# Placing stage of a graph network kernel: three of eight tiles picked on ScalarE, and SyncE's order of broadcasts and stores

## The chip, the cores and the metric

The kernel runs on one core of one Trainium2 chip. The time is device microseconds of one launch. Before the change three runs took 3246.53, 3248.45 and 3257.93 us; the median is 3248.45 us.

## The reference

100000 nodes with 64 features, 50000 edges (`src`, `dst`), `dst` sorted. A first layer takes a maximum over edges, a second one a normalised sum over edges, five times, each followed by a layer norm. Cut to what matters here:

```python
# layer 0: maximum over the edges of each target node
h = relu(concat([x[tgt], x[src] - x[tgt]], axis=1) @ W + b)
x = layernorm(x + maximum(segment_max(h, tgt), 0))
# layer 1: degree norm, then five sums over edges, mixed with six coefficients
deg  = segment_sum(ones, col);  inv = where(isinf(deg ** -0.5), 0, deg ** -0.5)
norm = inv[row] * inv[col]
for k in range(1, 6):
    tx = segment_sum(norm[:, None] * tx[col], row)
    result = result + coeffs[k] * tx
x = layernorm(x + result)
```

To do this in dense passes the kernel first sorts the edges by their first endpoint itself: it gives every edge a position, and writes the edge's record (64 features, two ids) to that position of a table in HBM. The stage that finds positions and writes records is the placing stage, and it alone is changed.

## The kernel before

`count_and_place` (L193) has four blocks of engine programs: reading the ids, counting, flags, and placing (L706 to L953). Then come a barrier and `edge_pass` and the sums.

**The data of the placing stage.** Edges stand in 392 tiles of 128. They are done four at a time, in 98 turns; turn (i, s) takes tiles of half s, with i from 0 to 48 and s 0 or 1. A node number is split in a high part (which of 250 rows) and a low part (which of 400 columns). `tps[s]` holds in PSUM, for half s, the next free position of every node (125 partitions, two times 400). Each turn of PE does, in this order:

- L858: for each of four tiles j, four matmuls of 400 columns pick the row of each edge's node out of `table[:, s]` into the bank `gps[j]`. The table is given in two bf16 parts, a high and a low one, for two halves of the rows. Ahead of tile j it waits for `got_read[j]`, that is, until the bank was read in the turn before.
- L836, ahead of tile 2: two matmuls take the high part away from `tps` of the other half, so that ACT can read the low part; and after tile 3 two more add the high part back for this half.
- L865: eight matmuls add the four tiles' one-hot rows to `tps[s]`, after `onehots[s]`; then `added[s]`.

**DVE** in a turn (L803): `ranks` of the next turn (L769, four comparisons with a row sum), `positions` of the turn before (L801, waits for all four `got_read` and writes `pos`), `hots` of the next turn (L779, L780, eight one-hot rows), then `pick` of this turn (L792): for each of four tiles it multiplies the 400 columns of `gps[j]` by the one-hot row of the low part and sums, which leaves the edge's position in `at[:, s, j]`.

**ACT** in a turn: `high` (L891, copies `tps` as bf16, after `added`), `rows` (L876 twice, L880: from a broadcast row `hibc` to the transposed one-hot rows `hiT`), `low` (L895), `factor` (L885, 32 numbers for each partition into `wide[s]`, after the load `wide_in[s]`, then `wide_ready[s]`).

**POOL** (L948) scatters four tiles by indirect DMA after `pos_ready`.

**SP** issues all plain DMAs of the stage from one in-order queue: `rows` (L725: two broadcasts `hibc` and `srcbc` of 256 KB, once `rows_used` from DVE's ranks and `dist_done` from ACT allow), `widened` (stores `wide[s]` to `x_ext`, after `wide_ready`), `widen` (loads `wide[s]` with node features, after `wide_stored`). A load or store is two DMAs, partitions 0 to 111 and 112 to 124 (`node_dma`, L127, so that their line in the profile is L130). This side job makes a copy of the node features with their factors, 100 pieces in all, and has nothing to do with the positions; it shares the ACT and SP programs. `wide` has two buffers.

Of the kernel before, what the change touches and what calls it, by code (L numbers as in the profile page):

```python
# [30 lines left out]
ACT = mybir.ActivationFunctionType  # L31
# [10 lines left out]
NEG = -1e30  # L42
ROUND = 12582912.0
FAR = float(1 << 20)

NP = 125
NC = N // NP
# [145 lines left out]
def count_and_place(nc, d, k):  # L193

    with ExitStack() as scope:
# [480 lines left out]
        front.close()  # L676
        two = lambda name: [sem(f"{name}{s}") for s in range(2)]
        rows_in, rows_used, dist_done, hiT_ready = two("rows_in"), two("rows_used"), two("dist_done"), two("hiT_ready")
        onehots, added, table_ready = two("onehots"), two("added"), two("table_ready")
        pos_ready = two("pos_ready")  # L680
        got, got_read = [sem(f"got{j}") for j in range(4)], [sem(f"got_read{j}") for j in range(4)]
# [5 lines left out]
        with ExitStack() as inner:  # L687
            isb = lambda name, shape, dt=FP32: inner.enter_context(nc.sbuf_tensor(name, shape, dt))
            hibc, srcbc = isb("hibc", [P, 2, GPOS]), isb("srcbc", [P, 2, GPOS])
            dist = isb("dist", [NP, 2, GPOS])  # L690
            hiT = isb("hiT", [NP, 2, 2, GPOS], BF16)
            ohp = isb("ohp2", [P, 2, 4, NROW], BF16)
            ohc = isb("ohc2", [P, 2, 4, NR], BF16)

# [14 lines left out]
            @block.sync  # L709
            def _(sp):  # L710
                by_column = (d.x.rearrange("(p c) f -> p c f", c=NC), d.x_ext[0:N, :].rearrange("(p c) f -> p c f", c=NC))

                def widen(i, s):
                    before, = settle(sp, k, i * 32)
                    sp.wait_ge(wide_stored[s], before)
                    cols = ds(i * (2 * KN) + s * KN, KN)
                    node_dma(sp, wide_in[s], lambda a, b: wide[a:b, s, :, 0:C], lambda a, b: by_column[0][a:b, cols, :])

                def widened(i, s):
                    again, = settle(sp, k, i + 1)  # L720
                    sp.wait_ge(wide_ready[s], again)
                    cols = ds(i * (2 * KN) + s * KN, KN)
                    node_dma(sp, wide_stored[s], lambda a, b: by_column[1][a:b, cols, :], lambda a, b: wide[a:b, s])

                def rows(i, s):  # L725
                    before, twice = settle(sp, k, i, i * 2)
                    sp.wait_ge(rows_used[s], before)
                    sp.wait_ge(dist_done[s], twice)
                    for to, of in ((hibc, d.hi_rows), (srcbc, d.src_rows)):
                        sp.dma_start(to[:, s], of[ds(i * GPOS + s * (ET // 2 * P), GPOS)].partition_broadcast(P)  # L730
                                     ).then_inc(rows_in[s], 16)

                for s in range(2):
                    rows(0, s)
                sp.dma_start(d.factor.rearrange("(p c) f -> p (c f)", c=NC), k.D[:]).then_inc(factor_stored, 16)
                sp.wait_ge(wide_blank, 1)
                for s in range(2):
                    widen(0, s)
                rows(1, 0)
                widened(0, 0)  # L740
                rows(1, 1)
                widened(0, 1)
                widen(1, 0)
                with sp.Fori(1, LAST) as i:
                    rows(i + 1, 0)
                    widened(i, 0)
                    widen(i, 1)
                    rows(i + 1, 1)
                    widened(i, 1)
                    widen(i + 1, 0)  # L750
                widened(LAST, 0)
                widen(LAST, 1)
                widened(LAST, 1)
                widen(LAST + 1, 0)
                widened(LAST + 1, 0)
                widen(LAST + 1, 1)
                widened(LAST + 1, 1)
                for s in range(2):
                    sp.wait_ge(wide_stored[s], (EB // 2 + 1) * 32)
                sp.wait_ge(factor_stored, 16)  # L760

            @block.vector
            def _(dve):
# [23 lines left out]
                def pick(i, s):  # L787

                    dve.wait_ge(onehots[s], i + 1)
                    for j in range(4):  # L790
                        dve.wait_ge(got[j], i * 2 + s + 1)
                        dve.scalar_tensor_tensor(picked[:, j], gps[j][:, 0:NR], 1.0, ohc[:, s, j],  # L792
                                                 ALU.mult, ALU.mult, accum_out=at[:, s, j:j + 1]
                                                 ).then_inc(got_read[j], 1)
# [36 lines left out]
            @block.tensor  # L831
            def _(pe):
                def high_part(s, sign):

                    for h in range(2):
                        last = pe.matmul(tps[s][:, h, 0:NR], eye[:, sign], table[:, s, 0, h],  # L836
                                         start=False, stop=True, skip_group_check=True)
                    return last

                for s in range(2):  # L840
                    for h in range(2):
                        last = pe.matmul(tps[s][:, h, 0:NR], k.ident[0:NP, 0:NP], start[:, s, h * NR:(h + 1) * NR],
                                         start=True, stop=True)
                last.then_inc(seeded, 1)
                pe.wait_ge(high_ready[0], 1)
                high_part(0, 1).then_inc(low_left[0], 1)
                with pe.Fori(0, EB // 2) as i:
                    for s in range(2):
                        pe.wait_ge(hiT_ready[s], i + 1)
                        pe.wait_ge(table_ready[s], i + 1)  # L850
                        for j in range(4):
                            if j == 2:
                                pe.wait_ge(high_ready[1 - s], i + s + 1)
                                high_part(1 - s, 1).then_inc(low_left[1 - s], 1)
                            pe.wait_ge(got_read[j], i * 2 + s)
                            for h in range(2):
                                for w in range(2):
                                    last = pe.matmul(gps[j][:, 0:NR], hiT[:, s, h, j * P:(j + 1) * P], table[:, s, w, h],  # L858
                                                     start=h + w == 0, stop=h + w == 2)
                            last.then_inc(got[j], 1)  # L860
                        high_part(s, 0)
                        pe.wait_ge(onehots[s], i + 1)
                        for j in range(4):
                            for h in range(2):
                                last = pe.matmul(tps[s][:, h, 0:NR], ohp[:, s, j, h::2], ohc[:, s, j],  # L865
                                                 start=False, stop=True, skip_group_check=True)
                        last.then_inc(added[s], 1)

            @block.scalar
            def _(act):  # L870
                def rows(i, s):

                    act.wait_ge(rows_in[s], i * 32 + 32)
                    act.wait_ge(hiT_ready[1 - s], i + s)
                    for h in range(2):
                        act.activation(dist[:, h], hibc[0:NP, s], ACT.Abs, bias=part[0:NP, h:h + 1]  # L876
                                       ).then_inc(dist_done[s], 1)
                    act.wait_ge(dist_done[s], i * 2 + 2)
                    act.wait_ge(added[s], i)
                    act.activation(hiT[:, s], dist[:], ACT.Relu, bias=1.0, scale=-1.0).then_inc(hiT_ready[s], 1)  # L880

                def factor(i, s):
                    act.wait_ge(wide_in[s], i * 32 + 32)
                    act.wait_ge(nd_ready, 1)
                    act.activation(wide[:, s, :, D_COL:], nd_all[:, ds(i * (2 * KN) + s * KN, KN), :], ACT.Copy  # L885
                                   ).then_inc(wide_ready[s], 1)
# [9 lines left out]

                for sign in range(2):
                    act.activation(eye[:, sign], k.ident[0:NP, 0:NP], ACT.Copy, scale=1.0 - 2.0 * sign)
                rows(0, 0)
                act.wait_ge(seeded, 1)  # L900
                high(0, 0)
                low(0, 0)
                with act.Fori(0, LAST) as i:
                    for s in range(2):
                        high(1 - s, i + s)
                        rows(i + s, 1 - s)
                        low(1 - s, i + s)
                        factor(i, s)
                high(1, LAST)
                rows(LAST, 1)  # L910
                low(1, LAST)
                factor(LAST, 0)
                high(0, LAST + 1)
                factor(LAST, 1)
                for s in range(2):
                    factor(LAST + 1, s)
# [1129 lines left out]
```

## Time and profile before

The profiled execution took 3252.13 us (its span is 3250.4 us), 3.7 us above the median of the three runs.

| engine | busy us | share of span |
|---|---|---|
| PE matmul | 1783.3 | 55% |
| DVE | 2578.0 | 79% |
| ACT | 1964.3 | 60% |
| POOL | 2228.1 | 69% |

The placing block runs from about 669 us to the first instruction of the next block at 1270.30 us. Shares over the whole span are means over many stages; for this change only the stretch of the placing stage is to be read, and in it which wait ends last.

### The profile page before, as it was taken

How to read it: one execution, taken by the hardware profiler on the slowest of the kernel's cores; microseconds unless marked ns; L12 is line 12 of the kernel's file. 1: busy time of each engine (PE TensorE's matmuls, PEld its weight loads, DVE VectorE, ACT ScalarE, POOL GpSimd, SP SyncE). 2: the span in 40 equal slices, each digit the busy share in tenths (PEclk: the TensorE clock that was granted, in tenths of full speed). 3: DMA queues.
4: the chain of work that ended last, by engine and by line, in shares of the span. 5: the costliest groups of instructions: out<-in, count | busy, mean ns of one | idle time of the engine just before them, and what ended most of it. 6: DMA issues, size and time to landing. Idle time of an engine off the chain costs nothing. (4 is left out here: it accounts for less than half of the span.)

```text
span 3250.4 us, 66637 instructions
## 1 busy us (share of the span) xinstructions
PE 1783.3 (55%) x9465; PEld 1075.8 (33%) x9465; DVE 2578.0 (79%) x12074; ACT 1964.3 (60%) x4437; POOL 2228.1 (69%) x2285
## 2 busy tenths in 40 slices
PE   7995555468888885988888883433333332000000
PEld 6884444335555553444444441111111111000000
DVE  8996999999999996899899996455556666555554
ACT  7995877556666663789888883255545400444443
POOL 6777777057777776577777775676666665777776
PEclk9998999989999997689888885555555555555555
DMA  4311444157777775688888885766667633222221
GB/s 142 109 24 23 116 109 108 52 142 202 204 203 203 204 202 126 170 211 221 203 214 212 214 208 112 175 177 181 174 156 202 169 92 79 69 69 70 74 74 53
DMA packets 736782, 467.28 MB, mean 144 GB/s; under 512 B 411287, under 2 KB 622546, under 8 KB 736728
## 3 DMA queue, kind: packets, MB, share of 16 engines
q1 hardware_dynamic: 636084, 321.23, 36.9%
q0 software_dynamic: 75296, 92.22, 13.3%
q10 hardware_dynamic: 25348, 53.33, 5.4%
q14 instruction: 48, 0.39, 0.0%
q8 instruction: 6, 0.10, 0.0%
HBM read 271.38 MB, written 197.86 MB: 144 GB/s over the span
## 5 line engine op out<-in xcount | busy, mean ns | idle before, releaser
L1647 POOL DMA_INDIRECT rows_H<-tab,at_H x424 | 404.2, 953 | 215.8 <-DVE at_H L1700 113.1
L948 POOL DMA_INDIRECT rec<-edge_x,pos x392 | 412.1, 1051 | 163.2 <-issue 159.3
L1150 POOL DMA_INDIRECT rows_M<-x_ext,at_M x400 | 379.4, 948 | 150.0 <-issue 100.0
L1922 POOL DMA_INDIRECT out_x<-res_L,to_L x384 | 374.2, 975 | 119.3 <-issue 107.0
L1668 ACT ACTIVATE node_H<-node_H,mean,M2n 125x64 f32<-125x64 f32 x800 | 273.6, 426 | 259.2 <-issue 152.6
L1808 PE MATMUL zT_H<-ident,z_H 128*64 128x128 f32 x496 | 150.3, 407 | 444.7 <-issue 351.9
L858 PE MATMUL gps<-table,hiT 125*128 125x400 bf16 x1568 | 300.8, 335 | 92.1 <-DVE picked L792 91.0
L377 POOL DMA_INDIRECT edge_x<-in_x,x_at x196 | 204.3, 1043 | 70.0 <-issue 58.8
L543 POOL DMA_INDIRECT edge_x<-in_x,x_at x196 | 187.7, 958 | 67.7 <-issue 59.4
L596 PE MATMUL aps<-ohc_f,ohp_f 128*125 128x400 bf16 x784 | 155.4, 341 | 130.3 <-DVE ohp_f L517 130.3
L1939 ACT ACTIVATE std_L<-M_L,coef 128x2 f32<-128x2 f32 x192 | 56.7, 295 | 274.9 <-DVE M_L L2001 274.7
L858 PEld LDWEIGHTS gps<-table,hiT 125*128 125x128 bf16 x1568 | 146.2, 98 | 222.6 <-DVE picked L792 125.3
L365 DVE TENSOR_SCALAR ohc<-iota,lo 128x400 bf16<-128x400 f16 x784 | 216.5, 317 | 0.0
L1808 PEld LDWEIGHTS zT_H<-ident,z_H 128*64 128x64 f32 x496 | 45.5, 140 | 484.7 <-issue 484.2
L792 DVE SCALAR_TENSOR_TENSOR picked<-gps,ohc 128x400 bf16<-128x400 f32 x392 | 200.4, 563 | 0.0
L449 PE MATMUL cps<-ohc,ohp 128*125 128x400 bf16 x784 | 198.1, 335 | 2.9 <-ACT ohd L414 2.6
L449 PE MATMUL cps<-ohc,ohd 128*125 128x400 bf16 x784 | 197.8, 334 | 0.0
L769 DVE SCALAR_TENSOR_TENSOR eq<-srcbc,recs,mask 128x128 bf16<-128x128 f32 (+3 forms) x392 | 194.1, 546 | 0.1
L891 ACT ACTIVATE table<-tps 125x800 bf16<-125x800 f32 x99 | 82.9, 837 | 170.6 <-PE tps L865 170.6
L1747 DVE TENSOR_TENSOR_SCAN sums_H<-cont,sums_H,zT_H 64x256 f32<-64x256 f32 (+1 forms) x248 | 182.2, 735 | 1.1 <-issue 0.6
L409 ACT ACTIVATE far<-iota,hi 128x250 f32<-128x250 f16 x392 | 163.6, 488 | 12.2 <-issue 12.2
L1157 POOL DMA_INDIRECT Ds<-factor,to x138 | 139.0, 1007 | 42.1 <-issue 41.5
(323 smaller groups left out, 5946.0 us busy)
## 6 DMA issues: line engine op xcount, KB each, us to landing
tab<-given_M SPq DMA_DIRECT2D x98, 384.0 KB
hibc_f<-dst_hi_rows SPq DMA_DIRECT2D x98, 256.0 KB
hibc<-hi_rows SPq DMA_DIRECT2D x98, 256.0 KB
srcbc<-src_rows SPq DMA_DIRECT2D x98, 256.0 KB
tab<-given_M SPq DMA_DIRECT2D x98, 256.0 KB
own<-given_M SPq DMA_DIRECT2D x98, 256.0 KB
own_L<-own SPq DMA_DIRECT2D x192, 128.0 KB
x_ext<-wide SPq DMA_DIRECT2D x100, 241.5 KB
```

Source lines behind the costliest of these rows:

```text
L365: last = dve.tensor_scalar(ohc[:, u, j, w], k.iota[:], lo[:, w, t], None, ALU.is_equal)
L377: pool.indirect_dma_start(out=edge_x[:, t // 4, t % 4, 0:C], out_offset=None, in_=d.x, in_offset=bass.IndirectOffsetOnAxis(ap=x_at[:, t:t ...
L449: last = pe.matmul(cps[2 if w else j // 2][:, h, 0:NR], rows[:, u, j, h::2], ohc[:, u, j, w], start=False, stop=True, skip_group_check=True)
L769: last = dve.scalar_tensor_tensor(eq[:, j, 0:n], srcbc[:, s, 0:n], recs[:, t, 1], mask[:, GPOS - n:GPOS], ALU.is_equal, ALU.mult, accum_ou ...
L792: dve.scalar_tensor_tensor(picked[:, j], gps[j][:, 0:NR], 1.0, ohc[:, s, j], ALU.mult, ALU.mult, accum_out=at[:, s, j:j + 1]).then_inc(got ...
L858: last = pe.matmul(gps[j][:, 0:NR], hiT[:, s, h, j * P:(j + 1) * P], table[:, s, w, h], start=h + w == 0, stop=h + w == 2)
L948: pool.indirect_dma_start(out=d.rec, out_offset=bass.IndirectOffsetOnAxis(ap=pos[:, s, j:j + 1], axis=0), in_=edge_x[:, i + s * (EB // 2), ...
L1150: pool.indirect_dma_start(out=rows[:, s, j, :], out_offset=None, in_=d.x_ext, in_offset=bass.IndirectOffsetOnAxis(ap=at[:, s, j:j + 1], ax ...
L1647: pool.indirect_dma_start(out=rows[:, s, j, :], out_offset=None, in_=gather, in_offset=bass.IndirectOffsetOnAxis(ap=at[:, s, j:j + 1], axi ...
L1668: last = act.activation(node[:, s, j], node[:, s, j], ACT.Identity, scale=k.M2n[:, col], bias=k.mean2[:, col])
L1808: last = pe.transpose(zT[s][:, j * P:(j + 1) * P], z[:, s, j, :], k.ident[:])
L1922: pool.indirect_dma_start(out=d.out, out_offset=bass.IndirectOffsetOnAxis(ap=to[:, s, j:j + 1], axis=0), in_=res[:, s, j, :], in_offset=No ...
```

## The change

PE adds, to the banks of three of eight tiles, 131072 times the one-hot row of the low part (one more matmul of 400 columns for each of them, with `lift`, a scaled unit matrix in bf16). The wanted column then stands 131072 above all others, and a relu of (value - 131072) with row sum on ACT gives the position. ACT does this for tiles 2 and 3 when s is 0 and for tile 3 when s is 1, between `low` and `factor`; DVE picks the others. PE now waits for `onehots[s]` ahead of the first lifted tile. In SP's program the broadcasts of a half are issued one half turn sooner: `rows(i+2, 0)` ahead of `widened(i, 1)` where `rows(i+1, 1)` stood, and so on. ACT makes `lift` and `lower` (the bias) once, at the start.

```diff
+LIFT = 131072.0
+ON_ACT = ((2, 3), (3,))
+ON_DVE = tuple(tuple(j for j in range(4) if j not in a) for a in ON_ACT)
@@ sync
                 rows(1, 0)
+                rows(1, 1)
                 widened(0, 0)
-                rows(1, 1)
+                rows(2, 0)
                 widened(0, 1)
                 widen(1, 0)
-                with sp.Fori(1, LAST) as i:
-                    rows(i + 1, 0)
+                with sp.Fori(1, LAST - 1) as i:
+                    rows(i + 1, 1)
                     widened(i, 0)
                     widen(i, 1)
-                    rows(i + 1, 1)
+                    rows(i + 2, 0)
                     widened(i, 1)
                     widen(i + 1, 0)
+                rows(LAST, 1)
+                widened(LAST - 1, 0)
+                widen(LAST - 1, 1)
+                widened(LAST - 1, 1)
+                widen(LAST, 0)
@@ vector, pick
-                    for j in range(4):
+                    for j in ON_DVE[s]:
@@ tensor
+                pe.wait_ge(lift_ready, 1)
...
-                                                     start=h + w == 0, stop=h + w == 2)
+                                                     start=h + w == 0, stop=h + w == 2 and j in ON_DVE[s])
+                            if j in ON_ACT[s]:
+                                pe.wait_ge(onehots[s], i + 1)
+                                last = pe.matmul(gps[j][:, 0:NR], lift[:], ohc[:, s, j], start=False, stop=True)
                             last.then_inc(got[j], 1)
@@ scalar
+                def pick(i, s):
+                    act.wait_ge(pos_ready[s], i)
+                    for n, j in enumerate(ON_ACT[s]):
+                        act.wait_ge(got[j], i * 2 + s + 1)
+                        act.activation(raised[:, n], gps[j][:, 0:NR], ACT.Relu, bias=lower[:],
+                                       accum_out=at[:, s, j:j + 1]).then_inc(got_read[j], 1)
+                act.activation(lift[:], k.ident[:], ACT.Copy, scale=LIFT).then_inc(lift_ready, 1)
+                act.activation(lower[:], k.ones[:, 0:1], ACT.Copy, scale=-LIFT).then_inc(lowered, 1)
...
                         low(1 - s, i + s)
+                        pick(i, s)
                         factor(i, s)
...
                 low(1, LAST)
+                pick(LAST, 0)
                 factor(LAST, 0)
                 high(0, LAST + 1)
+                pick(LAST, 1)
                 factor(LAST, 1)
```

## Rows read from the trace of the kernel before

**Rows 1.** Busy time by stretch: PE, PEld, DVE, ACT, POOL, clock, DMA share, GB/s
```profile
900.00:1000.00 100.00, 83.89 (x480) 53.47 (x479) 100.00 (x445) 68.31 (x104) 72.44 (x69) 1.00 0.77 204
```

**Rows 2.** Waits from 700 to 1240 us: who waited for whom, total, times, longest
```profile
ACT table L891 <- PE tps L865: 161.8, 92, 1.9
...
ACT wide L885 <- DMA wide<-in_x: 5.7, 15, 0.8
...
SPq L721 <- ACT wide L885: 198.0, 92, 3.2
```

**Rows 3.** Instructions in order of time, DVE in one turn: start, length, instruction, idle
```profile
903.03 0.56 DVE L792 SCALAR_TENSOR_TENSOR picked<-gps,ohc 128x400 bf16<-128x400 f32 x1
...
905.00 0.34 DVE L769 SCALAR_TENSOR_TENSOR eq<-srcbc,recs,mask 128x128 bf16<-128x128 f32 x1
...
906.89 0.15 DVE L801 TENSOR_TENSOR pos<-at,base 128x4 uint32<-128x4 f32 x1
...
908.89 0.56 DVE L792 SCALAR_TENSOR_TENSOR picked<-gps,ohc 128x400 bf16<-128x400 f32 x1
```

**Rows 4.** Instructions in order of time, ACT and PE in the same turn
```profile
902.74 0.84 ACT L891 ACTIVATE table<-tps 125x800 bf16<-125x800 f32 x1 [1.87 <-PE tps L865]
...
903.66 1.53 PE L858 MATMUL gps<-table,hiT 125*128 125x400 bf16 x8 [0.96 <-DVE picked L792]
...
905.79 0.82 ACT L895 ACTIVATE table<-tps 125x800 bf16<-125x800 f32 x1
...
906.50 0.22 ACT L885 ACTIVATE wide<-nd_all 125x32 f32 x1
...
908.61 0.84 ACT L891 ACTIVATE table<-tps 125x800 bf16<-125x800 f32 x1 [1.88 <-PE tps L865]
...
909.34 1.32 ACT L876 ACTIVATE dist<-hibc,part 125x512 f32<-125x512 f32 x2
```

**Rows 5.** Instructions in order of time, POOL at the end of the stage
```profile
1260.66 0.97 POOL L948 DMA_INDIRECT rec<-edge_x,pos  x1 [0.30 <-issue]
1261.93 0.97 POOL L948 DMA_INDIRECT rec<-edge_x,pos  x1 [0.31 <-issue]
```

**Rows 6.** Instructions in order of time, the factor on ACT and SP's issues
```profile
696.05 0.23 ACT L885 ACTIVATE wide<-nd_all 125x32 f32 x1 [0.24 <-DMA wide<-in_x]
...
696.51 0.93 SPq L130 DMA_DIRECT2D x_ext<-wide  x2
...
697.77 1.03 SPq L130 DMA_DIRECT2D wide<-in_x  x2
...
702.39 0.23 ACT L885 ACTIVATE wide<-nd_all 125x32 f32 x1 [0.35 <-DMA wide<-in_x]
...
725.04 0.23 ACT L885 ACTIVATE wide<-nd_all 125x32 f32 x1 [0.23 <-DMA wide<-in_x]
...
902.31 1.02 SPq L130 DMA_DIRECT2D wide<-in_x  x2
...
903.93 0.35 SPq L730 DMA_DIRECT2D hibc<-hi_rows  x1
```

**Rows 7.** Instructions in order of time, the same at the end of the stage
```profile
1252.71 0.99 SPq L130 DMA_DIRECT2D wide<-in_x  x2
...
1256.13 0.23 ACT L885 ACTIVATE wide<-nd_all 125x32 f32<-125x32 f32 x1 [4.37 <-DMA wide<-in_x]
...
1260.94 0.23 ACT L885 ACTIVATE wide<-nd_all 125x32 f32<-125x32 f32 x1 [4.57 <-DMA wide<-in_x]
```

**Rows 8.** Groups of ACT instructions by line and shape: busy, mean ns, idle before
```profile
L876 ACT ACTIVATE dist<-hibc,part 125x512 f32<-125x512 f32 x196 | 129.7, 711 | 5.8 <-DMA srcbc<-src_rows 5.8
...
L281 ACT ACTIVATE coef<-ones 128x1 f32<-128x1 f32 x1 | 0.2, 203 | 1.8 <-POOL ones L265 1.8
```

**Rows 9.** Instructions in order of time, a pair of broadcasts with nothing behind it
```profile
679.06 0.35 SPq L730 DMA_DIRECT2D hibc<-hi_rows  x1
```

**Rows 10.** Busy time by stretch, the end of that pair's transfers (columns of rows 1)
```profile
682.90:683.15 0.25, 0.25 (x3) 0.07 (x2) 0.25 (x3) 0.13 (x1) 0.19 (x1) 0.50 0.07 25
```

More of the change, by code:

```diff
@@ L678, in count_and_place @@
         rows_in, rows_used, dist_done, hiT_ready = two("rows_in"), two("rows_used"), two("dist_done"), two("hiT_ready")
+        lift_ready, lowered = sem("lift_ready"), sem("lowered")
         onehots, added, table_ready = two("onehots"), two("added"), two("table_ready")
@@ L691, in count_and_place @@
             hiT = isb("hiT", [NP, 2, 2, GPOS], BF16)
+            lift, lower = isb("lift", [P, P], BF16), isb("lower", [P, 1])
+            raised = isb("raised", [P, 2, NR])
             ohp = isb("ohp2", [P, 2, 4, NROW], BF16)
@@ L898, in _ @@
                     act.activation(eye[:, sign], k.ident[0:NP, 0:NP], ACT.Copy, scale=1.0 - 2.0 * sign)
+                act.activation(lift[:], k.ident[:], ACT.Copy, scale=LIFT).then_inc(lift_ready, 1)
+                act.activation(lower[:], k.ones[:, 0:1], ACT.Copy, scale=-LIFT).then_inc(lowered, 1)
                 rows(0, 0)
+                act.wait_ge(lowered, 1)
                 act.wait_ge(seeded, 1)
```

## The prediction

> **What bounds the kernel now.** I read the views from coarse to fine. Busy time by stretch comes first: in the placing stage DVE is busy 100.00 of 100 us, PE 83.89, POOL 72.44 and ACT 68.31, and PE runs at its full granted clock, 1.00 [rows 1]. So DVE has no idle time to give, and the others do. The list of waits says the same from the other side: ACT waits 161.8 us in 92 turns for PE's last matmuls [rows 2]. But ACT's list has a second line, which counts here: 15 times of 92 it waits for the load of `wide`, 5.7 us in all. And SP waits 198.0 us for ACT's factor [rows 2]. These two belong to one chain, and I come back to it.
>
> Then one turn in order of time. From pick to pick DVE's turn is 908.89 - 903.03 = 5.86 us [rows 3]. The four picks take from 903.03 to 905.00, that is 1.97 us or 0.49 us each (less than the 0.56 us of one instruction, since they overlap); the ranks take from 905.00 to 906.89, 1.9 us; the rest is positions and one-hot rows. ACT works from 902.74 to 906.72 (3.98 us) and then waits 1.88 us for PE [rows 4]. PE starts at 903.66, after 0.96 us of waiting for DVE's picks, and is done shortly before 908.61, when ACT's next copy starts [rows 4]: some 4.9 us for 28 matmuls, 0.17 us each. There are 98 turns.
>
> **The change part by part.**
>
> *DVE loses three picks of eight.* Two turns cost 11.72 us now, and 3 x 0.49 = 1.48 us go: 10.24 us, 5.12 us a turn in the mean. The edit has nothing else on DVE. If DVE stayed the bound, 95 turns in the loop would give 95 x 0.74 = 70 us. The question is what is late next.
>
> *PE gains three matmuls in two turns.* At 0.17 us each a turn has 28 plus 1.5, about 5.0 to 5.1 us. This takes up most of PE's idle time but stays below DVE's new 5.12. The new wait for `onehots[s]` costs nothing: DVE makes these rows ahead of the picks of the turn before, and PE itself waits for the first of those picks before it starts its turn [rows 4]. Behind that wait are the turn's other matmuls; nobody else is held.
>
> *POOL.* Where it is not kept waiting, its scatters follow each other by 1261.93 - 1260.66 = 1.27 us [rows 5]; four are 5.1 us. So POOL too could follow down to 5.1 and no further. It doesn't bind at a slower pace.
>
> *ACT gains three picks in two turns.* No relu with row sum is in the trace. The nearest row is L876, which has a bias operand as the pick has and 512 columns where the pick has 400: 0.711 us [rows 8], and the pair of them takes 1.32 us [rows 4], so that the first takes a slot of 0.61 us. Below that lies a half of the 800-column copy, 0.41 us [rows 4]. The row sum may be read out in an instruction of its own, as on DVE; the smallest ACT instruction takes 0.203 us [rows 8]. The bounds are thus 0.41 and 0.71 + 0.20 = 0.91 us; I take 0.7, near the slot of L876 with part of a read-out. ACT's turn is then 3.98 + 1.4 = 5.4 us with two picks and 4.7 with one, 5.8 and 4.9 at the upper bound. In the mean ACT is just below DVE's 5.12 too. ACT's 1.88 us of idle time covers the picks now; with a shorter turn the cover is all but used up.
>
> For this the rows say: a pick is 0.49 us on DVE and 0.6 or more on ACT, so moved work gets dearer, but it goes from an engine that never idles to one that waits 1.88 us a turn. The Trainium skill, page "ScalarE: Activation LUTs", section "Rules for kernel authors", advises VectorE and not ScalarE for a relu or a multiplication. By that rule alone the move would be a loss of 0.1 to 0.2 us an operation; the trace bears out the dearer price, and the busy shares speak for the move all the same.
>
> *The chain that becomes the bound: the side copy.* The factor of a turn needs the load of its `wide` buffer. SP issues that load only behind the store of the turn before, and this store waits for that turn's factor. So factor leads to factor: in the free-running start the factor ran at 696.05, the store was issued at 696.51, the next load at 697.77, and the next factor ran when it had landed, at 702.39 [rows 6]. The first part is 697.77 - 696.05 = 1.72 us and is the same in the new program. The landing took 4.62 us here. From 696.05 to 725.04 are five turns, each of which ended in such a wait; the first two and the last stand in [rows 6]; so the chain ran at 5.80 us a turn without being held by anything else, which leaves 4.08 us for a mean landing. At the end of the stage, with no broadcasts beside it, the landing took 1256.13 - 1252.71 = 3.42 us, and the whole chain 1260.94 - 1256.13 = 4.81 us [rows 7]. In mid-stage the load is issued at 902.31 and the factor comes at 906.50 without waiting, so it has landed within 4.19 us [rows 4, 6], as it had in 77 of 92 turns [rows 2].
>
> So this chain runs today at nearly the pace of DVE, 5.8 against 5.86 us; ACT's slack hides it. Once DVE and ACT could go at 5.1 it can't hide any more, because the factor now stands at the very end of an ACT program without slack, and the next `high` is queued behind it: then PE, then all others. The bounds of its turn are 1.72 + 3.42 = 5.14 us (nothing beside it) and 5.80 (the free start). The broadcasts are beside it all the time, so I stay near the upper end; but 77 of 92 turns without a wait show landings below the early mean. I take a landing of 3.98 us and a turn of 5.70 us.
>
> *SP's order.* The broadcasts of a half are needed by ACT at 909.34 and issued at 903.93 [rows 4, 6], 5.4 us ahead; at a turn of 5.70 they would have 0.3 us less in the old order. In the new order they have a turn more. What they are moved past is one store and one load. The kinds in the queue follow each other as before (broadcasts, store, load, broadcasts), only one half turn ahead in index, so each load still has the same bytes before it. The added wait is on `rows_used` of one turn later; queued behind it on SP are the store and the load. In a turn bound by the side chain DVE has 0.5 us of idle time and its ranks are done before SP comes to them, so I cost it at nothing; the second rival is what it costs otherwise.
>
> *Start and end.* Two small ACT instructions at the start (0.2 to 0.8 us) lie beside DVE's set-up. `rows(1, 1)` ahead of the first store may delay the side chain by a microsecond. At the end the side chain has three turns of about 4.8 us as before.
>
> **The sum.** 95 turns x (5.86 - 5.70) = 15 us. The profiled execution of 3252.1 us would become 3237; it lies 3.7 above the median of the runs, so against 3248.45 I forecast 3233 us. With 5.60 it is 25 us (3223), with 5.80 it is 6 us (3242).
>
> **The rivals.**
>
> *First: the side chain gives way (faster).* If the loads land in 3.4 to 3.8 us, as at the stage's end, the chain runs at 5.1 to 5.5 us, and DVE's 5.12, POOL's 5.1 or ACT set the pace. For it: 3.42 us [rows 7]. Against it: the early turns, and a DMA share of 0.77 that would rise to 0.85 or more in a shorter turn [rows 1]. Gain 95 x 0.36 to 0.74 = 34 to 70 us: 3178 to 3214. Chance 0.17.
>
> *Second: SP's new wait lands on the side chain (slower).* Today the ranks end at 906.89, 0.4 us after the factor at 906.50 [rows 3, 4]. If DVE keeps that lag, SP comes to the broadcasts, waits for the ranks, issues two broadcasts (about 0.9 us) and only then the store: 1.3 us after the factor in place of 0.46, so 0.9 us more in each turn of the chain. Worse, the store's data could queue behind the broadcasts': a lone pair issued at 679.06 was still moving at 682.9 [rows 9, 10], almost 4 us, of which up to 3 would lie ahead of the store. The full price can't persist, since a turn longer by so much lets DVE catch up; a quarter to a half microsecond over today's turn could. This decides from the point where the broadcasts are issued less than about 3 us ahead of the store. At 6.0 to 6.3 us a turn it costs 13 to 42 us: 3261 to 3290. Against it: nothing in the sum keeps DVE late, once it has slack. Chance 0.18.
>
> The Trainium skill, page "DMA: Bandwidth & Descriptors", section "Queues, rings and completion order", says that each DMA engine takes its descriptors in ring order. By that rule broadcasts issued just ahead of a store do stand before it, which is what this rival needs; no row here shows the order by itself.
>
> *Third: ACT's picks are dear, or the chain stays at its early pace (no change).* At 0.91 us a pick the turn with two is 5.8 us and the other is bound by the load at 5.7 to 5.8: 3240 to 3252. Chance 0.15.
>
> **How the numbers follow.** The forecast's own case, a turn of 5.60 to 5.80 us, has 0.50 and spans 3223 to 3242; the first rival 0.17, the second 0.18, the third 0.15. A measurement of this kernel can tell about 0.5% from no change, that is 16 us, or 3232. The forecast's case is cut in half by that line. Faster: 0.17 + 0.25 = 0.42. Within 0.5%: 0.25 + 0.15 = 0.40. Slower: 0.18. The range of 8 in 10 leaves out about half of each outer rival: 3195 to 3266.
>
> **What would show it.** In the new profile the turn from `high` to `high` should be 5.7 us; DVE's busy share in the stage should fall to about 90% and it should wait for ACT's picks or PE; ACT's wait for PE should nearly vanish and its wait for the load of `wide` should grow from 5.7 us to tens of us in most turns; an ACT pick should be near 0.6 to 0.7 us. If instead DVE stays at 100% with a turn near 5.15, the first rival is right. If the broadcasts are issued right after the end of DVE's ranks and the store right behind them, with a load landing over 4.5 us after its issue, it is the second. What would make me wrong is above all the landing time of the load: 0.1 us of it is 9.5 us of the result.

## The result, and the profile after

The changed kernel takes 3226.69 us (median of 7 runs, 3216.22 to 3234.35), the kernel before 3248.45 us (median of 7). The ratio is 0.9927, with a 95% interval of 0.9904 to 0.9949: about 24 us faster, between 17 and 31. The forecast was 3233 us, 15 us faster.

The placing block, from its first POOL instruction to the first one of the next block, went from 1270.30 - 669.42 = 600.9 us to 1243.50 - 669.65 = 573.9 us in the profiled executions, 27.0 us. The first instruction of the next block, before and changed (start, length, instruction, idle before it):

```profile
1270.30 0.10 POOL L1163 MEMSET d_got_M<- 128x3 f32 x1 [7.39 <-POOLq L97]
...
1243.50 0.10 POOL L1192 MEMSET d_got_M<- 128x3 f32 x1 [9.03 <-POOLq L100]
```

The two spans differ by 34.4 us. The other 7 us lie in blocks that the change doesn't touch; more on that at the end. The profiled execution of the changed kernel, 3217.72 us, is also 9 us shorter than the median of its runs. A turn, from one `high` of ACT to the next, took 5.86 us in the mean and takes 5.61 (90 turns from 702.67 to 1207.53 us); 95 turns of that are 24 us, and the other 3 of the 27 us lie ahead of these turns or behind them.

Busy time by stretch, changed kernel, columns as in rows 1:

```profile
900.00:1000.00 100.00, 92.07 (x526) 58.23 (x524) 92.60 (x411) 86.46 (x161) 72.19 (x73) 1.00 0.76 212
```

DVE is no longer full. PE rose from 84 to 92 us and ACT from 68 to 86. POOL did not move, 72.19 for 72.44, although its scatters in 100 us rose from 69 to 73, as the shorter turns want: one of them is shorter now, 0.99 us in the mean for 1.05. The waits from 700 to 1230 us (who waited for whom, total, times, longest), first of PE, ACT, DVE and POOL, then SP's:

```profile
POOL rec L977 <- issue: 128.4, 365, 3.3
PEld tps L848 <- ACT table L914: 71.0, 89, 2.2
ACT wide L908 <- DMA wide<-in_x: 61.1, 74, 2.2
...
DVE pos L813 <- ACT raised L902: 33.9, 38, 2.2
POOL rec L977 <- DVE pos L813: 14.6, 17, 1.5
```

```profile
SPq L727 <- ACT wide L908: 177.4, 94, 3.2
```

ACT's 161.8 us of waits for PE [rows 2] are gone, and the line for the load of `wide` has grown from 5.7 us in 15 turns to 61.1 us in 74. What stands behind it in the list is its echo: PE waits for ACT's `high`, which is queued behind the factor; DVE waits for ACT's picks. Two turns in order of time, ACT and SP:

```profile
899.19 1.02 SPq L133 DMA_DIRECT2D wide<-in_x  x2
...
901.37 0.59 ACT L902 ACTIVATE raised<-gps,lower 128x400 f32<-128x400 f32 x1
901.85 0.20 ACT L902 ACTIVATION_READ_ACCUMULATOR raised<-gps,lower 128x1 f32 x1
903.73 0.23 ACT L908 ACTIVATE wide<-nd_all 125x32 f32 x1 [1.68 <-DMA wide<-in_x]
904.04 0.84 ACT L914 ACTIVATE table<-tps 125x800 bf16<-125x800 f32 x1
904.16 0.92 SPq L133 DMA_DIRECT2D x_ext<-wide  x2
...
905.40 1.00 SPq L133 DMA_DIRECT2D wide<-in_x  x2
...
907.80 0.59 ACT L902 ACTIVATE raised<-gps,lower 128x400 f32<-128x400 f32 x1
...
908.37 0.59 ACT L902 ACTIVATE raised<-gps,lower 128x400 f32<-128x400 f32 x1
...
909.12 0.23 ACT L908 ACTIVATE wide<-nd_all 125x32 f32 x1
909.25 0.82 ACT L914 ACTIVATE table<-tps 125x800 bf16<-125x800 f32 x1
```

The turn with one pick waits for its load: issued at 899.19, factor at 903.73, a landing of 4.54 us ("landing" is the time from the issue of the load to the factor that waited for it). This one is long: in the 74 turns that waited the mean is 3.97 us, from 3.34 to 5.11. The turn with two picks has ACT at work from 904.04 to 909.25 without a gap, 5.21 us. From factor to load issue it is 905.40 - 903.73 = 1.67 us (mean of 95 turns 1.68, and 1.68 in the kernel before in the same stretch; [rows 6] has 1.72). The two picks with their read-outs take 909.12 - 907.80 = 1.32 us, 0.66 each.

### The profile page after: what moved, and what is told of

Read it like the earlier page. It is cut to its first block and busy times, and to the rows that moved or that the text cites. A ratio compares the mean times of both kernels' runs of the same rounds, so it can differ in the third digit from the quotient of the medians.

```text
span 3216.0 us, 67050 instructions
## 1 busy us (share of the span) xinstructions
PE 1807.6 (56%) x9612; PEld 1089.5 (34%) x9612; DVE 2510.0 (78%) x11780; ACT 2051.7 (64%) x4733; POOL 2210.8 (69%) x2285
## 5 line engine op out<-in xcount | busy, mean ns | idle before, releaser
L977 POOL DMA_INDIRECT rec<-edge_x,pos x392 | 398.5, 1016 | 148.3 <-issue 131.2
L871 PEld LDWEIGHTS gps<-table,hiT 125*128 125x128 bf16 x1568 | 153.2, 98 | 109.3 <-issue 3.4
L1737 DVE SCALAR_TENSOR_TENSOR value_H<-rows_H,coef 128x128 f32<-128x128 f32 x212 | 73.3, 346 | 113.1 <-DMA rows_H<-tab,at_H 112.0
L559 ACT ACTIVATE dist_f<-hibc_f,part 125x512 f32<-125x512 f32 x196 | 130.8, 714 | 41.3 <-DMA hibc_f<-dst_hi_rows 35.2
```

Of the source, the lines that this page charges most:

```text
L977: pool.indirect_dma_start(out=d.rec, out_offset=bass.IndirectOffsetOnAxis(ap=pos[:, s, j:j + 1], axis=0), in_=edge_x[:, i + s * (EB // 2), ...
```

## The experiments

The ratios are to runs of the kernel before on the same chip. "Turn" is the mean of 90 turns of ACT; "stage" is the placing block as above, in the profiled execution; "scatters" is from the first to the last start on POOL's scatter line. Two kernels that leave the fourth tile's scatters for later ran once each and are read for their turns only.

| kernel | ratio to before (95%) | turn us | stage us | scatters us |
|---|---|---|---|---|
| before | 1 | 5.86 | 600.9 | 570.8 |
| changed | 0.9927 (0.9904 to 0.9949) | 5.61 | 573.9 | 543.2 |
| picks_only | 1.0034 (1.0010 to 1.0059) | 6.02 | 613.3 | 584.3 |
| order_only | 0.9993 (0.9974 to 1.0013) | 5.87 | 601.6 | 570.7 |
| two_picks | 0.9903 (0.9877 to 0.9930) | 5.64 | 576.2 | 545.4 |
| load_first | 0.9914 (0.9883 to 0.9945) | 5.54 | 568.3 | 539.3 |
| two_picks_load_first | 0.9892 (0.9858 to 0.9927) | 5.52 | 567.0 | 536.9 |
| deep_pos | 0.9849 (0.9823 to 0.9874) | 5.47 | 564.4 | 535.4 |
| three_buffers | 0.9883 (0.9863 to 0.9903) | 5.51 | 565.3 | 536.2 |
| three_buffers_deep_pos | 0.9911 (0.9893 to 0.9928) | 5.12 | 569.8 | 540.7 |

### The two halves of the change

**picks_only**: the picks are moved, SP keeps the order of the kernel before.

> Only the picks are moved; SP keeps its old order. Side-chain theory: the chain of the side copy is the same and runs at 5.6 us a turn; the broadcasts come 5.4 us ahead at a turn of 5.86 and 5.1 us ahead at 5.6, with a landing of about 5 us, so ACT waits for some of them, 0 to 0.3 us a turn: ratio 0.993 to 0.999. Rival, the new order brings most of the gain: ratio 1.000 or above. Rival, the new order is of no use: 0.9927 as the whole change.

It is slower than the kernel before, 1.0034, where 0.993 to 0.999 was expected: the number is that of the rival in which the new order brings the gain. The wait was foreseen, its price wasn't: ACT and DVE both wait for the broadcasts, in most turns.

```profile
DVE eq L775 <- DMA srcbc<-src_rows: 66.2, 75, 1.9
ACT dist L886 <- DMA srcbc<-src_rows: 65.2, 70, 1.9
```

(Waits of picks_only from 700 to 1200 us.) The lead, from the issue of the broadcasts to ACT's first use, was 5.48 us in the mean before ([rows 4, 6] show one of 5.4), and 2 of 85 turns waited. Here it is 4.74 us and 70 turns wait. In the old order the broadcasts stand behind the store and the load, these stand behind the factor, and the factor now stands behind the picks.

**order_only**: DVE picks all tiles, SP has the new order.

> Only SP's order is changed; DVE picks all eight tiles. DVE stays the bound at 5.86 us a turn. Theory of the prediction's second rival: DVE's ranks end 0.4 us after the factor, so the broadcasts and behind them the store are issued up to 0.9 us later than now; the side chain then takes 5.8 + 0.3 to 0.9 us and takes the pace over: turn 5.9 to 6.2, ratio 1.002 to 1.010. Rival, the wait costs nothing since ACT's slack of 1.9 us covers a later load: turn 5.86, ratio 1.000.

No change, 0.9993. The place of the second rival was right and its price was wrong. Waits from 700 to 1200 us, SP's first, then ACT's:

```profile
SPq L728 <- DVE eq L775: 101.0, 84, 2.0
```

```profile
ACT wide L891 <- DMA wide<-in_x: 148.2, 85, 2.4
```

SP does wait 101 us for DVE's ranks before it issues the broadcasts, and ACT's waits for the load rose from 5.1 us in the same stretch to 148.2. But ACT had 149.4 us of idle time in it, ahead of `high`, and this covers the whole: the turn is 5.87 us with DVE at 100%. Of that idle time 1.1 us is left, so the cover is used up to the last. Neither half gains by itself, and the order is what makes the moved picks pay.

### How many picks

**two_picks**: `ON_ACT = ((3,), (3,))`.

> The changed kernel with only tile 3 on ACT in every turn (two of eight). DVE then needs 5.37 us a turn, ACT 4.7. Side-chain theory: the landing of the load still sets the pace, turn 5.5 to 5.65, ratio 0.990 to 0.994, as the whole change; ACT's waits for the load grow to 80 us or more. Rival, the picks on ACT are the cost: turn 5.37 to 5.4, 20 us below the changed kernel, ratio 0.986.

The turn is 5.64 us for 5.61, and ACT's waits for the load are 86.3 us in the 500 us from 700 to 1200, where the changed kernel has 58.3. Every turn waits for its load here: 1.69 us from factor to load issue and a landing of 3.92 us in the mean make 5.61. The ratio, 0.9903, can't be told from the changed kernel's. So the third pick brings little, 2.3 us of the stage: what DVE saves goes into waiting for the load.

### The load off the factor's chain

**load_first**: the changed kernel with

```diff
                     rows(i + 1, 1)
-                    widened(i, 0)
                     widen(i, 1)
+                    widened(i, 0)
                     rows(i + 2, 0)
-                    widened(i, 1)
                     widen(i + 1, 0)
+                    widened(i, 1)
```

> The changed kernel, but SP issues each load of wide ahead of the store of the other buffer and behind the broadcasts, so the load no longer waits for the same turn's factor (it needs only the store of a turn before). Side-chain theory: the load has landed long before its factor, ACT's 59 us of waits for it vanish, and the turn drops from 5.60 us to what DVE (5.12), POOL (5.1) or ACT (5.4 and 4.7 with and without a second pick) allow, about 5.2 us: 30 to 38 us below the changed kernel, ratio to the kernel before 0.980 to 0.985. Rival, ACT with its picks sets the pace: the waits vanish but the turn stays at 5.5 to 5.6, ratio 0.991 to 0.993. Rival, the DMA engines themselves are full: loads land later instead, turn 5.6, ratio 0.993.

ACT's waits for the load fell from 58.3 to 1.6 us in these 500 us, as the side-chain theory said, but the turn only to 5.54 us and the stage to 568.3, not by the 30 us expected. Turn and ratio are those of the rival with ACT's picks, but its cause is not what the trace shows (and three_buffers_deep_pos, below, has the same picks at 5.12 us a turn). The median turn fell from 5.54 to 5.18 us; 72 of 90 turns were now 4.9 to 5.7 us, and three were over 10. One of these in order of time, POOL and DVE's positions:

```profile
840.60 1.05 POOL L977 DMA_INDIRECT rec<-edge_x,pos  x1 [0.31 <-issue]
...
845.90 0.99 POOL L977 DMA_INDIRECT rec<-edge_x,pos  x1 [4.26 <-issue]
...
853.41 0.16 DVE L813 TENSOR_TENSOR pos<-at,base 128x4 uint32<-128x4 f32 x1 [4.42 <-DMA rec<-edge_x,pos]
```

POOL stood still for 4.26 us between two scatters, and DVE, which has two position buffers, waited 4.42 us for a scatter to land. The same pause of POOL is in every kernel here with four scatters a turn, after scatters 113, 225 and 337 of 392; in the kernel before, the starts are 3.26 us apart there. There POOL makes it up; here it can't, because it has almost no idle time left (4.6 us of waits for positions in these 500 us).

**two_picks_load_first**:

> Load ahead of the store, and only tile 3 on ACT in every turn: DVE needs 5.37 us a turn, ACT 4.7. Theory, POOL's 535 us bind with three picks of eight as well: the stage is 0 to 6 us longer than with three picks (568 to 574 us), ratio to the kernel before 0.990 to 0.993. Rival, ACT's picks and PE's turn bind there: the stage is as long or shorter, 560 to 568 us, ratio 0.988 to 0.990.

The stage is 567.0 us, 1.3 us less than with three picks, and the turn 5.52. By the numbers on record that is the rival's band, but 1.3 us part the two kernels, and this run can't tell them apart. What it shows is that the third pick isn't needed here either. Long runs of its turns are 5.37 us, DVE's sum with two picks moved; the three pauses and their aftermath make up the rest.

### Is it POOL?

**deep_pos**: load_first with a position buffer for each turn, so that DVE never waits for a scatter:

```diff
-            pos = isb("pos", [P, 2, 4], U32)
+            pos = isb("pos", [P, EB, 4], U32)
...
-                    dve.wait_ge(scattered[s], i * 64)
-                    dve.tensor_tensor(pos[:, s], at[:, s], base[:, s], ALU.add).then_inc(pos_ready[s], 1)
+                    dve.tensor_tensor(pos[:, ds(i * 2 + s, 1)], at[:, s:s + 1], base[:, s:s + 1], ALU.add).then_inc(pos_ready[s], 1)
```

> The order with the load ahead of the store, and a buffer of positions for every turn in place of two, so that DVE never waits for a scatter to land. In the run before this one DVE waited 33 us for scatters and PE 57 us (weight loads) for DVE. Theory, POOL's own work is now the bound (392 scatters at 1.27 us and more, 535 us from the first to the last): the stage gets shorter by 0 to 5 us only, 563 to 568 us from its first POOL instruction to the next block's, DVE's waits for scatters vanish but POOL stays behind DVE. Rival, the coupling of the engines by the two buffers costs the turn: the stage gets shorter by 15 to 25 us, 545 to 553 us. Ratio to the kernel before 0.989 to 0.991, or 0.983 to 0.986.

The stage is 564.4 us, 3.9 below load_first: the first theory's band. The ratio, 0.9849, is the other theory's; the extra is outside the stage (last section). The turn was 5.47, still above what the engines need. The waits of SP and of ACT from 700 to 1200 us point at the reason:

```profile
SPq L721 <- DMA x_ext<-wide: 159.9, 92, 2.6
```

```profile
ACT wide L907 <- DMA wide<-in_x: 44.6, 56, 2.3
...
DVE eq L781 <- DMA srcbc<-src_rows: 23.0, 37, 1.5
```

My swap had made a chain of its own. The load now waits for the last store to land, and the next store is queued behind the load.

**late_fourth**: deep_pos, with the scatters of every fourth tile after the loop.

> As deep_pos, and POOL scatters only three of the four tiles of a turn in the loop and the 98 fourth ones after it, so POOL needs 3.9 us a turn. All results are still written; the 98 scatters at the end add about 125 us to the stage. Only the turn counts. Theory, POOL was the bound at 5.3 to 5.5 us a turn: the turn drops to what ACT, PE and DVE allow, 5.1 to 5.2 us. Rival, POOL wasn't the bound: the turn stays at 5.4 to 5.5 us.

The turn drops to 5.24 us (90 turns from 700.26 to 1171.79, one run), between the two expectations, and POOL waits 150.6 us for DVE where it had waited 0.9. In deep_pos no engine waits for a scatter, so POOL can lengthen the turn only by what its work does to the others. Both waits for DMAs fell:

```profile
ACT wide L907 <- DMA wide<-in_x: 32.5, 46, 3.9
...
DVE eq L781 <- DMA srcbc<-src_rows: 8.3, 16, 0.9
```

That is 27 us less in 500 us, and 90 turns are 21 us shorter. So the 0.2 us a turn fit the scatters' load on the DMAs; that this is the cause is argued and not shown.

**late_fourth_after**: the same on the changed kernel's own SP order.

> The changed kernel in its own order of loads and stores, with positions for every turn and the fourth tile's scatters after the loop, as in late_fourth. Side-chain theory: the load behind the store sets the pace and POOL has nothing to do with it, so the turn stays at 5.5 to 5.65 us and ACT's waits for the load stay at 55 us or more. Rival, POOL sets the pace of the changed kernel too: turn 5.1 to 5.3 us.

5.57 us for 5.61 (one run). Here POOL is out of the way and the turn stays, with 56.3 us of ACT's waits for the load. In the changed kernel's loop the side chain sets the pace.

**three_buffers**: the changed kernel, a third buffer of `wide`, each load issued two turns ahead; SP's and ACT's loops written out:

```diff
-            wide = isb("wide", [NP, 2, KN, EXTW])
+            wide = isb("wide", [NP, 3, KN, EXTW])
...
+                for t in range(EB + 2):
+                    if t + 3 < EB:
+                        rows((t + 3) // 2, (t + 3) % 2)
+                    widened(t)
+                    if t + 2 < EB + 2:
+                        widen(t + 2)
```

> The changed kernel with three buffers of wide in place of two, each load issued two turns ahead of its factor (behind the store, as in the change); SP's and ACT's loops are written out. In the run with the load ahead of the store the chain of the side copy was only replaced: each load there waits for the landing of the last store, 112 to 160 us in 500 us. Here it waits for a store of a turn earlier. Side-chain theory: ACT's waits for the load fall below 5 us, SP's waits for landings of stores as well, and the stage falls from 574 us to POOL's and DVE's pace with two position buffers, 560 to 567 us, turn 5.2 to 5.45 us. Rival, picks on ACT and the banks between PE and ACT set the pace: 570 to 574 us.

ACT no longer waits for a load at all, SP no longer for stores, and the stage is 565.3 us, as expected; the turn, 5.51 us, is a little above the band. Its median is 5.22, and three turns after POOL's pauses take over 10 us, as in load_first. DVE waits 28.7 us for scatters to land and PE after it. The third buffer and the written-out loops came together and no run parts them; but load_first reaches a median turn of 5.18 us with the loops as they were.

**three_buffers_deep_pos**: both.

> Three buffers of wide and in addition positions for every turn. Theory: with the side chain and the coupling to POOL both gone, DVE, PE and ACT run at 5.1 to 5.2 us a turn and POOL, at 392 scatters of 1.27 us with 8 to 12 us of stalls, at 520 to 535 us from first to last scatter, is the bound: stage 553 to 563 us, 11 to 21 us below the changed kernel's 574, and turns clearly shorter than 5.47. Rival, broadcasts or the DMA engines' load hold the turn at 5.4 and more: stage 563 to 567 us as with deep positions alone.

The turn came out as the theory had it, the stage did not: 553 to 563 us were expected, with scatters of 520 to 535, and it is 569.8 with 540.7. That settles what bounds the stage. The whole list of waits from 700 to 1200 us, without SP's, and the busy time as in rows 1:

```profile
POOL rec L959 <- issue: 121.2, 361, 4.5
ACT table L896 <- PE tps L862: 27.1, 47, 0.7
PEld gps L852 <- DVE picked L786: 23.8, 70, 0.5
ACT wide L890 <- DMA wide<-in_x: 4.2, 1, 4.2
ACT raised L883 <- PE gps L856: 3.0, 1, 3.0
DVE pos L794 <- ACT raised L883: 1.5, 1, 1.5
DVE picked L786 <- PE gps L852: 0.7, 2, 0.4
```

```profile
900.00:1000.00 100.00, 99.32 (x578) 64.42 (x577) 100.00 (x451) 93.59 (x179) 77.75 (x74) 1.00 0.86 232
```

DVE is full again. DVE, ACT and PE run at 5.12 us a turn, exactly DVE's sum in the prediction; and the stage is 569.8 us, longer than with turns of 5.47. POOL never waits for a position once the stage is running:

```profile
L959 POOL DMA_INDIRECT rec<-edge_x,pos x392: 966/972/1508, 689.7 to 1230.4; - x196
...
  issue: 130.3, 391
  DVE pos L794: 2.6, 1
```

(The scatters: shortest, median and longest in ns, first and last start in us; then what ended POOL's idle time.) The 392 scatters take 540.7 us with nothing to wait for, 1.38 us each. They bind: DVE writes its last positions at 1182 us, 48 us before POOL's last scatter. That the stage is 5 us longer than in deep_pos fits the scatters too: their instructions take 411.1 us in all for 404.9.

## Why the prediction was right, and which step was mis-sized

*DVE's three picks, 0.49 us each.* Right: 5.12 us a turn with DVE at 100%, measured in three_buffers_deep_pos.

*PE's three matmuls, its wait for the one-hot rows and ACT's picks.* PE's bound was right but has no room in it (in three_buffers_deep_pos PE is busy 99.32 of 100 us, at turns of 5.12; and 4.9 us for 28 matmuls make 5.16 us for 29.5, not 5.0 to 5.1). The new wait cost nothing. A pick was priced at 0.7 us and is 0.66 with its read-out, 0.59 plus 0.20 less their overlap. The two-pick turn is 5.21 us where I had 5.4.

*The side chain.* It was named as the next bound, with 1.72 us plus a landing, and it is: ACT's waits for the load, the unchanged turn with two picks or with POOL out of the way, and the end of these waits when the load is taken off the chain. The landing was taken as 3.98 us, and in the 74 turns that waited for it it is 3.97: right, with luck in the last digit, since the rows gave 3.42 to 4.62. What was mis-sized is the turn of 5.70 as a mean over all turns. The first part is 1.68 us and not 1.72, and 21 of 95 turns did not wait for their load at all: it had landed within 3.71 us in the mean, and ACT's own work ended the turn. Over all 95 turns the time from load issue to factor is 3.91 us; with 1.68 that is 5.59, and 5.61 is measured. So the term was too large by 0.09 us of 5.70; in 95 turns it is 9 us, as much as the miss from 15 to 24. Part of that agreement is luck, since the 24 us are known to 7.

*SP's order.* The sentence that the broadcasts would have "0.3 us less" in the old order was too mild. Their lead falls by 0.7 us, from 5.48 to 4.74, although the turn gets no shorter, since their issue stands behind the factor too: picks_only has turns of 6.02 us. That the added wait on the ranks is covered was right in the changed kernel. In order_only the wait is there, 101 us of it, and costs nothing either.

*POOL.* Here a step was wrong without harm to the number. I priced a scatter at 1.27 us from the quiet end of the stage [rows 5] and said POOL could follow down to 5.1 us a turn. In the busy stage it takes 1.38 us with all waits removed, so 5.5 us a turn. So of the first rival's 34 to 70 us only the lowest part could be had: 95 x (5.86 - 5.5) = 34 us, and the shortest stage here, 564.4 us in deep_pos, is 36.5 us less than before. The changed kernel is near that bound already: its scatters take 543.2 us, 535.4 in deep_pos and 540.7 in three_buffers_deep_pos. The prediction has the side chain as the one bound; it sets the turn, but POOL stands 0.1 us a turn behind it.

*What would show it.* A turn of 5.7 (5.61), DVE at about 90% (92.6), ACT's waits for PE gone (they are) and its waits for the load in most turns (74 of 94): each came as written.

**A version that beats both.** deep_pos takes 0.9849 (0.9823 to 0.9874) of the kernel before. Its interval lies clear of the changed kernel's. In its stage it gains 9.5 us on the changed kernel; the ratios differ by 25 us, and how much of the rest will stay is open.

## What to carry to other kernels

Before you take work off the full engine, list every chain that its slack now hides, with the pace of each. Here there were three close behind (a load behind a store behind a small ACT instruction at 5.6 to 5.8 us a turn, the scatters at 5.5, the broadcasts' lead), and after 0.25 us of gain the next one was there. An engine's pace is to be read where the stage is busy and nothing holds the engine, not at its quiet end. And when a wait is moved, look at what is queued behind it: my own swap of load and store removed one chain and made another.

## What the runs showed of the hardware that was not expected

- POOL's scatters of 128 rows follow each other at 1.27 us in quiet and at 1.38 us in the mean of a stage in which DVE and the DMAs are busy (three_buffers_deep_pos, 540.7 us for 391 intervals). Of the 41 us between the two some 30 are longer instructions (91 of 392 take over 1.1 us, up to 1.51, for a median of 0.97), and 11 are three pauses of some 4 us, the first after 113 scatters and the next after 112 more each. After DVE's last positions at 1182 us the intervals are 1.28 us again. Whether DVE, the DMAs or something else lengthens them wasn't tried.
- The pauses have an idle time of 2.3 us each in the kernel before, and of 3.6 to 4.9 us in the five kernels with the shortest stages. In the two kernels that leave the fourth scatter for later they come after nearly the same counts (113, 224, 335) and are 1.5 to 2.1 us. Their cause is open.
- ACT's relu with row sum is two instructions, 0.59 us for 400 columns and 0.20 us for the read-out, and takes 0.66 us of ACT.
- The unchanged block behind the placing stage isn't equally long in all executions: its row gathers took 682.0 us from first to last start in the kernel before, 678.8 in the changed one, 691.1 in load_first, 694.3 in three_buffers, 676.6 in three_buffers_deep_pos and 672.2 in deep_pos. That is as much as the effects studied here, and it is why the stage's own length stands beside each ratio. Its cause is open.
